# A two-layer cross-attention and expert kernel on one core: three queues in new order, at the head, at the routing, and in the units of the last stage

## The reference, cut to what matters

```python
x = x + tanh(g_xattn[0]) * _L0_xattn_ref(_layernorm(x), ctx, Wq, Wk, Wv, Wo)
x = x + tanh(g_ffn[0])   * _L0_ffn_ref(_layernorm(x), w1s, w2s, w3s, W1, W2, W3, Wg)
x = x + tanh(g_xattn[1]) * _L1_xattn_ref(ctx, ctx, _layernorm(x), Wk, Wv, bv, Wq, bq, Wo, bo)
x = x + tanh(g_ffn[1])   * _L1_ffn_ref(_layernorm(x), W_exp, b_exp, up_weights, ...)

# layer 0, attention: inside each row, over its own 16 x 16 numbers (DK = NH = 16)
Q = (x @ Wq.T).reshape(b, length, 16, 16).swapaxes(-2, -1)      # K, V alike, of ctx
attn = softmax(einsum('blih,bljh->blij', Q, K) / sqrt(16))
concat = einsum('blij,bljh->blih', attn, V).swapaxes(-2, -1).reshape(b, length, 256)
return concat @ Wo.T

# layer 0, feed-forward: one shared expert, and the best of 8
idx = argmax(xf @ Wg, axis=-1)
return geglu(xf, w1s, w2s, w3s) + sum_e where(idx == e, geglu(xf, W1[e], W2[e], W3[e]), 0)

# layer 1, attention: the usual one, 512 rows against 512 context rows, one head of 256
probs = softmax(einsum('bqd,bkd->bqk', qp, kp) / sqrt(256))
return einsum('bqk,bkd->bqd', probs, vp) @ Wo.T + bo

# layer 1, feed-forward: 256 -> 1024, 10 butterfly stages, gelu, 10 butterfly stages, -> 256
h = butterfly(x @ W_exp + b_exp, up_weights)
return butterfly(gelu(h + up_bias), down_weights) @ W_con + b_con + down_bias
```

## Time and profile before

| | before |
|---|---|
| median of 3 runs | 731.09 us (726.58 to 732.46) |
| the profiled execution's own time | 731.78 us |
| its span, from first to last recorded instruction | 730.0 us |
| TensorE busy | 685.3 us (94%) |
| VectorE busy | 621.5 us (85%) |
| GpSimd busy | 427.1 us (59%) |
| ScalarE busy | 411.5 us (56%) |

### The profile page before, as it was taken

How to read it: one execution, slowest core, us unless ns; L and a number is a source line. 1 busy time by engine, 2 the same in 40 slices (tenths; PEclk the granted TensorE clock), 3 DMA queues, 4 the chain that set the end, 5 groups by cost and what they waited for, 6 DMA issues and landing times.

```text
span 730.0 us, 12948 instructions
## 1 busy us (share of the span) xinstructions
PE 685.3 (94%) x4385; PEld 590.0 (81%) x4385; DVE 621.5 (85%) x914; ACT 411.5 (56%) x762; POOL 427.1 (59%) x305
## 2 busy tenths in 40 slices
PE   6639999999999899899999999999987999999998
PEld 5429888888888799667778888888875899999997
DVE  5697999999999935699999999999887877787664
ACT  2424455554554421466768877777744666456653
POOL 3897999999999972211999766679231211220000
PEclk9968999999999999999999999999999999999999
DMA  8601110111137012333255416110010111000000
GB/s 272 238 8 30 51 30 29 29 35 48 32 104 301 9 66 73 100 124 129 89 202 197 178 59 253 30 30 23 8 44 14 45 31 58 30 30 9 9 16 29
DMA packets 28658, 56.43 MB, mean 77 GB/s; under 512 B 3424, under 2 KB 24672, under 8 KB 27456
## 3 DMA queue, kind: packets, MB, share of 16 engines
q1 hardware_dynamic: 23424, 47.64, 18.1%
q0 software_dynamic: 1872, 5.11, 2.5%
q10 hardware_dynamic: 3312, 3.02, 1.2%
HBM read 48.55 MB, written 7.21 MB: 76 GB/s over the span
## 4 chain that ended last, share of the span: by engine, by line
PE 43%; DVE 12%; issue 5%; ACT 4%; POOL 3%; DMA 0%; POOLq 0%; DVEq 0%; ACTq 0%
PE bank L758 18%; PE bank L749 8%; PE bank L1032 8%; PE bank L766 4%; PE bank L1137 2%; POOL PRODV L631 2%; DVE PRODV_r L2063 1%; DVE STC L2152 1%; PE bank L1220 1%; PE bank L818 1%; ACT XST L1568 1%; DVE SHARED_r L2063 1%; ACT SLOT_r L1541 1%; ACT SLOT_r L1572 1%; DVE MVC L2154 1%
## 5 line engine op out<-in xcount | busy, mean ns | idle before, releaser
L631 POOL TENSOR_TENSOR PRODV<-SHARED 128x2048 f32<-128x2048 f32 x32 | 144.6, 4518 | 8.2 <-DVE bank L1754 5.6
L749 PE MATMUL bank<-ROWS,SLOT 128*128 128x128 f32 x1024 | 124.8, 281 | 0.4
L749 PEld LDWEIGHTS bank<-ROWS,SLOT 128*128 128x128 f32 x1024 | 120.2, 196 | 2.9 <-ACT G L1288 2.8
L723 POOL TENSOR_TENSOR RS<-VE,MHALF 128x2 f32<-128x2 f32 x15 | 12.4, 825 | 141.1 <-DVE VE L2159 141.1
L633 POOL TENSOR_TENSOR PRODV<-PRODV 128x1024 f32<-128x1024 f32 x32 | 74.8, 2337 | 2.5
L1673 DVE TENSOR_TENSOR PRODQ<-bank,SHARED 128x4096 f32<-128x4096 f32 x16 | 70.8, 4423 | 4.8 <-PE bank L749 4.1
L1682 DVE TENSOR_REDUCE bank<-PRODQ 128x256 f32<-128x4096 f32 x16 | 70.7, 4420 | 0.1
L664 POOL DMA_INDIRECT XS<-normal_rows,INV x23 | 28.8, 1251 | 66.9 <-PE bank L766 48.6
L2063 DVE TENSOR_TENSOR PRODQ_r<-SLOT,ROWS_r 128x1024 fp32r<-128x1024 f32 x44 | 62.2, 1446 | 0.0
L2063 DVE TENSOR_TENSOR W_r<-SLOT,PRODQ_r 128x1024 fp32r<-128x1024 f32 x44 | 58.6, 1332 | 1.8 <-ACT PRODQ_r L1441 1.8
L818 PE MATMUL bank<-SLOT,HA 128*128 128x256 f32 x256 | 59.9, 384 | 0.0
(11 more groups left out here) (294 smaller groups left out, 1915.8 us busy)
## 6 DMA issues: line engine op xcount, KB each, us to landing
SLOT<-wexp SPq DMA_DIRECT2D x9, 3072.0 KB, 11.4
SHARED<-ctxT SPq DMA_DIRECT2D x16, 128.0 KB, 2.4
ROWS<-xT SPq DMA_DIRECT2D x16, 128.0 KB, 2.2
normal_rows<-ROWS SPq DMA_DIRECT2D x16, 128.0 KB, 1.7
WET<-ctxT SPq DMA_DIRECT2D x4, 512.0 KB, 8.4
out<-X SPq DMA_DIRECT2D x16, 128.0 KB, 1.7
X<-x SPq DMA_DIRECT2D x15, 128.0 KB, 2.5
expert_rows<-YS ACTq DMA_DIRECT2D x12, 128.0 KB, 1.7
```

What stands on the lines that cost most here:

```text
L631: gp.tensor_tensor(o, pr, v, ALU.mult).then_inc(s["av_prod"], 1)
L749: last = pe.matmul(dst, lhs(k), rhs(k), start=(k == 0), stop=(k == chunks - 1))
```

## The change

It has three parts.

1. **Head.** GpSimd computes the first tile's root ahead of its last growth step rather than behind it. The value biases leave GpSimd: `value_bias` is gone, and ScalarE writes the two tiles at the start of `pair_products`, which now stands behind the exponential of the first tile's scores and no longer ahead of it.
2. **Routing.** TensorE multiplies the ranks in the middle of tile b's down products. VectorE adds tile b's shared rows behind the one-hot tables rather than ahead of the places, and copies INV ahead of the experts of the tiles.
3. **Units of the last stage, VectorE.** Where there is a next unit, the split of its values and queries stands ahead of the attended rows of the second tile and their guard. In the last unit the attended rows and their guard stand ahead of the last quarter of the hidden split.

```diff
--- before.py
+++ after.py
@@ -588,33 +588,24 @@
                 settle()
                 run(gp.tensor_tensor(dst.rearrange("p (c o r) -> p c o r", c=KF, o=2), cf, v, ALU.mult))
 
-            def grown_up():
+            def grown_up(t0):
 
                 gp.wait_ge(coef_in[0], 16)
                 v = COEF[0][:, 0:16]
                 for k in range(1, LOW):
+                    if k == LOW - 1:
+                        first_root(t0)
                     w = GROW[:, 1 - k % 2, 0:16 << k]
                     grow_up(k, v, w)
                     v = w
                 settle()
                 gp.nop().then_inc(e_up, 1)
 
-            def value_bias():
-
-                gp.wait_ge(exact, 6)
-                gp.wait_ge(c_in, 16 * 5)
-                for k in range(KD):
-                    gp.tensor_scalar(BVB[:, k, :], rounded(ONES[:, :]), BV[:, k:k + 1], 1.0, ALU.mult, ALU.mult)\
-                        .then_inc(bvb_ready, 1)
-
             def step(of):
                 if (t3 := of(3)) is not None:
                     second_root(num(t3))
                 if (t0 := of(0)) is not None and first(t0, 1):
-                    grown_up()
-                    first_root(t0)
-                elif t0 is not None and first(t0, 2):
-                    value_bias()
+                    grown_up(t0)
                 if (t1 := of(1)) is not None:
                     n, par = num(t1), t1[1]
                     gp.wait_ge(s["exp_done"], n + 1)
@@ -955,8 +946,9 @@
                 normal_rows(c)
                 down_rows(b, 0, 1)
                 gate(c)
-                down_rows(b, 1)
+                down_rows(b, 1, 5)
                 ranks()
+                down_rows(b, 5)
                 up_half(c, 0)
                 up_half(c, 1)
                 inverse()
@@ -1367,8 +1359,6 @@
                     act.activation(KV[:, t0[1], at], PB[4][:, at], ACT.Copy).then_inc(s["kv_sb"], 1)
                     if first(t0, 1):
                         row_sums(t0)
-                    elif first(t0, 2):
-                        pair_products()
                 if t3 is not None:
                     less_mean(t3)
                 if t1 is not None:
@@ -1380,6 +1370,8 @@
                         act.wait_ge(s["sums"], n1 - 1)
                     act.activation(PR[:, t1[1], :], SC[:, :], ACT.Exp, scale=ROW1[:, t1[1], 3:4])\
                         .then_inc(s["exp_done"], 1)
+                if t0 is not None and first(t0, 2) and not first(t0, 1):
+                    pair_products()
                 if t3 is not None:
                     scaled_rows(t3)
                     normal_rows(t3)
@@ -1391,6 +1383,11 @@
 
             def pair_products():
 
+                act.wait_ge(c_in, 16 * 5)
+                act.wait_ge(consts, 6)
+                for k in range(KD):
+                    act.activation(BVB[:, k, :], IDENT[:, :], ACT.Identity, scale=0.0, bias=BV[:, k:k + 1])\
+                        .then_inc(bvb_ready, 1)
                 for n, (dst, src) in enumerate(((WQ1[:, :, :].rearrange("p k d -> p (k d)"), PB[6][:, :]),
                                                 (WV1[:, :, :].rearrange("p k d -> p (k d)"), PB[7][:, :]),
                                                 (BK[:, :], PB[2][:, 0:KD]))):
@@ -1837,13 +1834,13 @@
                 second_norm(c)
                 mult(b, 1)
                 choices()
-                add_shared(b)
                 places()
                 mult(c, 0)
                 one_hots()
+                add_shared(b)
                 mult(c, 1)
+                inverse()
                 expert_of_tiles()
-                inverse()
                 slots_of_tiles()
                 add_shared(c)
 
@@ -2250,14 +2247,17 @@
                     next_rows(u + 2)
                     next_stats(u + 2)
                 lower_hidden(u - 1, 2)
-                lower_hidden(u - 1, 3)
-                attended(2 * u + 1)
-                norm_eps(u, 2, "d_agg", "d_eps")
+                if has_next:
+                    lower_hidden(u - 1, 3)
                 if has_values:
                     for r in range(2):
                         lower_values((u + 1) // 2, r)
                 if has_next:
                     lower_queries(u + 1)
+                attended(2 * u + 1)
+                norm_eps(u, 2, "d_agg", "d_eps")
+                if not has_next:
+                    lower_hidden(u - 1, 3)
                 norm_rows(u, 2, "d_rstd", "d_xT", "d_xn")
                 if has_second:
                     norm_rows(u + 2, 0, "c_rstd", "c_xT", "c_xn")
```

## The result

The changed kernel takes 733.37 us, the median of 19 runs between 730.88 and 736.61. The kernel before, run beside it 19 times, has 731.09 us (726.58 to 733.61). The ratio of the new times to the old is 1.0033, with a 95% interval from 1.0021 to 1.0045: slower by a third of a per cent, some 2.4 us. The forecast was no change, 731.0 us. The time lies in the wide range of 725.2 to 735.0, a little above the forecast's own 728.5 to 733, and the measurement tells it from no change, on the slow side.

The account below looks back on a forecast made before the run. TensorE was taken to set the pace, with VectorE and GpSimd close behind. Terms -3.2 - 0.6 + 2.7 + 0.1 + 1.2 + 0.1 - 0.4 = -0.1 from 731.09 gave 731.0 us, own range 728.5 to 733, wide range 725.2 to 735.0.

Parts of the forecast that it names:

- The head, -3.2: Start of kernel: GpSimd's first value product starts at 19.9 instead of 23.17, so TensorE's long wait ends earlier; -3.2 us.
- The routing, -0.6: Before the first gather: INV copied ahead of the experts of the tiles, so gathered rows come earlier; -0.6 us.
- The chain of the units: Last stage: splits first delay VectorE's attended rows through row maximum, so TensorE's flips of the weights wait; +3.7 in all.
- Into unit 3: Last stage: the split waits for ScalarE's rounded queries, so attended rows and all behind them come 1.37 us later.
- Into unit 2: Last stage: the 1.3 us wait for the queries' split goes, but a wait at the flip replaces it; +0.1 us.
- the steps into 3, 5 and 7: Last stage, steps without values to split: VectorE's chain delayed 1.37 us twice, then +0.1 for the last step.
- the steps into 2, 4 and 6: Last stage: VectorE's delayed chain costs +0.1 for the first step, and 0.6 each for the two where values are split.
- The last unit, -0.4: End of last stage: attended rows before the fourth hidden split remove up to 0.9 us of wait, partly returned; -0.4 us.
- a rival with a chance of 12%: Last stage: TensorE's clock falls in the pauses into units 3 and 5, 1.5 us each; 734.0 us, chance 12%.
- The rival that the reordering helps: Last stage: VectorE's chain does not hold the flips, so the reordering gains 2.2 us; 725.1 us, chance 15%.
- The one that the head's gain is absorbed: Head: TensorE's start hangs on something unmoved, or GpSimd's products are stretched, so 3.2 us come back; 734.2 us, chance 13%.

Follow-up runs that it names:

- the even units with filled pauses: Kernel before with head and routing edits, splits first only in steps into units 3, 5, 7, plus extra transpositions in the two long pauses: 730.39 us, ratio 0.9990.
- the even units: Kernel before with head and routing edits, and the splits ahead of the attended rows only in the steps into units 3, 5 and 7: 734.05 us, ratio 1.0037.
- pauses filled: Changed kernel plus 34 extra TensorE transpositions ahead of its waits for the exponential in units 2 to 6: 731.79 us, ratio 0.9999.
- the head alone: Kernel before with only the head's part of the diff: 727.72 us, ratio 0.9956.
- the units alone: Kernel before with only the new order of VectorE's units in the last stage: 737.95 us, ratio 1.0081.
- the odd units: Kernel before with head and routing edits, and the splits ahead of the attended rows only in the steps into units 2, 4 and 6: 727.33 us, ratio 0.9964.

## Why the prediction was wrong

**The head, -3.2.** Right in place and size: -3.2 us by the times, between 1.3 and 5.0, and 3.22 in the trace. That the trace has the forecast's 19.9 almost to the digit is in part luck. The forecast let GpSimd's queue end last; in the changed kernel's profile GpSimd was done at 17.80, and the exponential came last, because VectorE shifted the scores at 18.91 and not at 18.23. The Trainium skill's remark on the interfaces that GpSimd shares with VectorE (GPSIMD Engine Reference, section 8) was set against this term; the moved product took 4.50 us where it had taken 4.51, so no part of the gain was lost that way. It was no test of the rule: beside the product VectorE summed scores before (one input) and multiplied scores after, with one input in SBUF and the other in a bank, so no instruction with two SBUF inputs ran beside it.

**The routing, -0.6.** The copy for INV came 0.73 us sooner after the start of its product, within the bounds of 0 and -0.8. The times can't confirm a gain; the traces of the experiments have some 0.5 us at the first gathered rows.

**The chain of the units.** Right in mechanism and near in every size. Into unit 3 the forecast was 1.37 and the trace has 1.36. Into unit 2 it was 0.1: 582.51 less 588.03 is -5.52, and the flips of the first normalized rows, which lie ahead of that step, stand at 565.67 before and at 560.09 after, -5.58, so the step cost 0.06. For the steps into 3, 5 and 7, the even units with filled pauses cost 2.6 us by the times and 2.89 by the trace where 2.8 stood in the sum. For the steps into 2, 4 and 6 the sum had 1.3, the times 0.7 and the trace 1.42. The idle times on VectorE stand where they were put, ahead of the split and between guard and normalized rows.

**The last unit, -0.4.** In the trace a wait of 0.9 became one of 0.4, and the rest of the stage is 0.56 us shorter; in the times it is not to be seen. Nothing speaks against the number.

**The step that failed** is the clock of TensorE in the new pauses: the sum has no term for it, and it was left to a rival with a chance of 12%. It was the case: filling the new pauses takes 0.34% off the changed kernel, 2.5 us, and 0.47% off the one with the even units, 3.4 us. With the pauses filled the changed kernel's ratio is 0.9999, which is the forecast's -0.1, so nothing else that the times could tell is missing from the sum. The rival's price was sound, 1.5 us a fall against 1.55 measured. But its pause was put at about 1.8 us, made of the delay of 1.37, the old wait of 0.25 and 0.2 for TensorE's earlier start; TensorE came to it earlier than that, and the pause was 2.05. The forecast's own rows had 2.13 us with a fall behind it and 1.46 without, and 2.05 lies next to the former. And it was treated as a switch that is on or off. The changed kernel's profile has one fall behind two equal pauses, and a forecast must take such a cost as a frequency times a price. One to two falls of 1.55 us turn the sum of -0.1 into +1.5 to +3.0; +2.4 was measured.

**The rival that the reordering helps** (725.1) fell: the flips wait, 7.1 us in all. The one that the head's gain is absorbed (734.2) gives nearly the measured time for a wrong reason: the head alone gained its 3.2 us.

## What to carry to other kernels

Where a chain of small steps on one engine feeds the next unit's bound engine, the step with another engine's round trip in it (here the root between guard and normalized rows) goes first, and independent work goes behind it to cover the trip; moving that work ahead removed a wait of 1.3 us here and made five others. Count not only how long the bound engine then pauses but what the pause does to its clock: a fall behind a pause of 2 us cost some 1.6 us more, and it came in five of the six cases in the profiles of the changed kernel, the units alone and the even units. Idle time of TensorE that can't be removed can be filled with matmuls that nobody reads, so long as they end before the wait does.

## What the runs showed of the hardware

Work that nobody reads made this kernel faster. In short stretches that hold no change of it, TensorE's granted clock was either 1.00 or 0.50.

Counted over the profiles of all twelve kernels between 60 and 700 us, it fell around a pause of 2.05 to 2.15 us in 13 of 16 cases: 8 of 10 at the end of the first stage, 5 of 6 in the last stage. Pauses of 1.2 to 1.55 us in these stretches were never followed by a fall, the five of up to 1.4 us in the last stage of the odd units among them. The length of the pause alone does not decide, though. Near 540 us a pause of 1.68 us was followed by a fall in the kernel with the head alone, and pauses of that length in six other kernels were not; in the changed kernel one of 2.32 us was not, while one of 2.54 (pauses filled) and one of 2.83 (units alone) were. And in the profile of the units alone the clock fell at 294 us, where TensorE's only pause in the 35 us ahead was one of 0.17. The wait and the window of the first case, then the windows of the changed kernel behind its pause of 2.12 and of the units alone at 294 us:

```profile
540.35 0.41 PE L1259 MATMUL bank<-IDENT,SLOT 128*128 128x128 f32 x2 [1.68 <-DVE SLOT L2296]
...
541.30:544.60 3.30, 3.22 (x13) 2.50 (x14) 1.45 (x3) 1.18 (x3) 0.00 (x0) 0.50 0.00 0
...
250.70:254.40 3.70, 3.70 (x30) 3.60 (x31) 1.36 (x4) 2.04 (x4) 3.70 (x1) 1.00 0.71 229
...
294.30:297.90 3.60, 3.60 (x10) 2.86 (x10) 2.33 (x13) 0.00 (x0) 1.83 (x2) 0.53 0.08 16
```

In the head the clock still fell at 50 us, behind a pause of 1.58 us, in a kernel in which the pauses ahead had been filled. With 88 transpositions added in old pauses the mean clock went from 0.986 to 0.994 and the time from 727.53 to 725.46 us. The clock also goes with much of the spread from run to run: the runs of the changed kernel with a mean clock of 0.988 took 730.9 and 731.4 us, those with 0.974 took 736.1 and 736.5.
